# Two units of a graph layer's aggregation, one after the other or matmul by matmul in turn

## The reference

```python
h = relu(layernorm(x))                        # over the nodes
q, k = einsum('c,bcn->bn', wq, h), einsum('c,bcn->bn', wk, h)
scores = q[:, None, :] + k[:, :, None]        # then leaky relu, slope 0.01
att = softmax(scores, axis=-1)                # 1024 x 1024 a batch
agg = einsum('bcn,bmn->bcm', h, att)
out = x + relu(einsum('oc,bcm->bom', adj, agg) + bm)
```

## Time and profile before

| | |
|---|---|
| Time, median of 3 runs | 2122.78 us (2120.24 to 2122.8) |
| Profiled execution: time, span | 2123.36 us, 2121.6 us |
| TensorE matmuls busy | 2055.9 us (97%), 11312 instructions |
| VectorE busy | 1640.8 us (77%) |
| ScalarE busy | 1219.2 us (57%) |
| GpSimd busy | 390.6 us (18%) |
| Mean granted TensorE clock | 0.993 of full |

### The profile page before, as it was taken

The page is one execution under the profiler, slowest core; times in us unless marked ns, Lnnn a source line. Parts: engine busy times, 40 slices in busy tenths (PEclk is TensorE's granted clock), DMA queues, the critical chain, the costliest instruction groups (busy, mean ns, idle before and its releaser), DMA issues.

```text
span 2121.6 us, 35163 instructions
## 1 busy us (share of the span) xinstructions
PE 2055.9 (97%) x11312; PEld 960.5 (45%) x11312; DVE 1640.8 (77%) x3661; ACT 1219.2 (57%) x1873; POOL 390.6 (18%) x266
## 2 busy tenths in 40 slices
PE   4599999999999999999999999999999999999999
PEld 2244444444444444444444444444444444444444
DVE  6777788778888778787777887787887777877753
ACT  3565555655646665556655556555566655566543
POOL 0012211112212112111122211122111122111221
PEclk9799999999999999999999999999999999999999
DMA  5265544555544565444565445555445654445541
GB/s 169 91 149 140 125 106 144 134 149 139 117 102 152 128 156 135 100 123 140 139 148 120 118 129 136 144 139 118 105 149 129 154 134 104 120 143 139 114 100 40
DMA packets 178624, 271.51 MB, mean 128 GB/s; under 512 B 87648, under 2 KB 87648, under 8 KB 170336
## 3 DMA queue, kind: packets, MB, share of 16 engines
q1 hardware_dynamic: 178528, 270.59, 50.1%
HBM read 202.91 MB, written 67.63 MB: 128 GB/s over the span
## 4 chain that ended last, share of the span: by engine, by line
PE 80%; DVE 10%; issue 7%; DMA 1%; ACT 1%; SPq 0%; DVEq 0%; POOLq 0%
PE mix L338 15%; PE mix L339 15%; PE mix L340 15%; PE mix L319 10%; PE mix L321 10%; PE mix L320 10%; DVE den_out L612 4%; DVE p_ring L632 4%; PE small L302 2%; DVE p_lo L639 2%; DMA ab_rows<-ab_col 1%; DMA wm_nat<-in_adj_dram 0%; ACT v_hi L426 0%; DVE v_lo L644 0%; DMA ab_row<-ab_rows 0%
## 5 line engine op out<-in xcount | busy, mean ns | idle before, releaser
L338 PE MATMUL mix<-p_hi,v_hi 128*128 128x512 f16 x2048 | 777.2, 379 | 10.1 <-DVE p_lo L639 10.1
L339 PE MATMUL mix<-p_lo,v_hi 128*128 128x512 f16 x2048 | 776.9, 379 | 0.0
L340 PE MATMUL mix<-p_hi,v_lo 128*128 128x512 f16 x2048 | 776.8, 379 | 0.0
L736 POOL TENSOR_TENSOR res<-res,y 128x512 f32<-128x512 f32 x256 | 386.1, 1508 | 1710.2 <-ACT y L433 1710.2
L414 ACT ACTIVATE p_ring<-ab_row,cols 128x512 f32<-128x512 f32 x512 | 349.4, 692 | 181.4 <-DVE p_lo L639 155.4
L632 DVE SCALAR_TENSOR_TENSOR p_ring<-ab_row,cols,p_ring 128x512 f32<-128x512 f32 x512 | 376.7, 747 | 77.1 <-ACT p_ring L414 46.5
L319 PE MATMUL mix<-wmT_hi,h_hi 128*128 128x512 f16 x1024 | 389.2, 380 | 0.0
L321 PE MATMUL mix<-wmT_hi,h_lo 128*128 128x512 f16 x1024 | 389.1, 380 | 0.0
L320 PE MATMUL mix<-wmT_lo,h_hi 128*128 128x512 f16 x1024 | 389.1, 380 | 0.0
L612 DVE SCALAR_TENSOR_TENSOR den_out<-den_row,cols 128x512 f32<-128x512 f32 x512 | 371.6, 762 | 0.0
L422 ACT ACTIVATE p_hi<-p_ring 128x512 f16<-128x512 f32 x512 | 303.2, 592 | 87.3 <-DVE p_ring L632 69.9
(11 more groups left out here) (56 smaller groups left out, 782.2 us busy)
## 6 DMA issues: line engine op xcount, KB each, us to landing
xs<-in_x_dram SPq DMA_DIRECT2D x128, 512.0 KB, 6.1
res<-in_x_dram SPq DMA_DIRECT2D x256, 256.0 KB, 3.5
out_dram<-res SPq DMA_DIRECT2D x256, 256.0 KB, 2.5
den_row<-den_rows SPq DMA_DIRECT2D x32, 1024.0 KB, 4.6
ab_row<-ab_rows SPq DMA_DIRECT2D x32, 1024.0 KB, 6.8
wm_nat<-in_adj_dram SPq DMA_DIRECT2D x1, 1024.0 KB, 9.7
den_rows<-cols SPq DMA_DIRECT2D x32, 8.0 KB, 1.6
ab_rows<-ab_col SPq DMA_DIRECT2D x32, 8.0 KB
```

The costliest lines, as they stand in the source:

```text
L338: pe.matmul(ps[:, :], v_hi[:, nt, chans], p_hi[:, hf, nt, :], start=(nt == 0), stop=False)
L339: pe.matmul(ps[:, :], v_hi[:, nt, chans], p_lo[:, hf, nt, :], start=False, stop=False)
L340: mm = pe.matmul(ps[:, :], v_lo[:, nt, chans], p_hi[:, hf, nt, :], start=False, stop=(nt == NT - 1))
L736: pool.tensor_tensor(res[:, k, :], res[:, k, :], y[:, k % 2, :], ALU.add).then_inc(s_add, 1)
```

## The change

`unit` becomes `unit_pair`: units k and k + 1 run together. In each node tile the two take turns matmul by matmul, in two banks, with the same moving tile of p and different weight tiles of v. Both banks are waited for ahead of the pair, and each unit raises `s_acc` with its last matmul. The number of matmuls is the same, and so is their order within a unit; no other engine's program is touched.

```diff
-            def unit(b, k):
-                hf, ot = divmod(k, OT)
-                if k < MIX:
-                    pe.wait_ge(s_vlo[k % 2], cnt(b, NT // 2, (k + MIX) // 2 + 1))
-                else:
-                    pe.wait_ge(s_y[k % 2], cnt(b, U // 2, (k - MIX) // 2 + 1))
-                ps, chans = mix[k % MIX], slice(ot * P, (ot + 1) * P)
+            def unit_pair(b, k):
+                hf = k // OT
+                pair = (k, k + 1)
+                for u in pair:
+                    if u < MIX:
+                        pe.wait_ge(s_vlo[u % 2], cnt(b, NT // 2, (u + MIX) // 2 + 1))
+                    else:
+                        pe.wait_ge(s_y[u % 2], cnt(b, U // 2, (u - MIX) // 2 + 1))
                 for nt in range(NT):
                     if k == 0:
                         pe.wait_ge(s_vlo[nt % 2], cnt(b, NT // 2, nt // 2 + 1))
-                    if ot == 0:
+                    if k % OT == 0:
                         pe.wait_ge(s_plo, cnt(b, G, NT * hf + nt + 1))
-                    pe.matmul(ps[:, :], v_hi[:, nt, chans], p_hi[:, hf, nt, :], start=(nt == 0), stop=False)
-                    pe.matmul(ps[:, :], v_hi[:, nt, chans], p_lo[:, hf, nt, :], start=False, stop=False)
-                    mm = pe.matmul(ps[:, :], v_lo[:, nt, chans], p_hi[:, hf, nt, :],
-                                   start=False, stop=(nt == NT - 1))
-                mm.then_inc(s_acc, 1)
+                    for v, p in ((v_hi, p_hi), (v_hi, p_lo), (v_lo, p_hi)):
+                        for u in pair:
+                            ot = u % OT
+                            mm = pe.matmul(mix[u % MIX][:, :], v[:, nt, ot * P:(ot + 1) * P], p[:, hf, nt, :],
+                                           start=(nt == 0 and v is v_hi and p is p_hi), stop=(nt == NT - 1 and v is v_lo))
+                            if nt == NT - 1 and v is v_lo:
+                                mm.then_inc(s_acc, 1)
 
             def period(b, one, two):
-                for k in range(U):
-                    unit(b, k)
+                for k in range(0, U, 2):
+                    unit_pair(b, k)
```

## The result

The kernel with pairs takes 2139.6 us (median of 4 runs, 2138.99 to 2140.6), the kernel before on the same chip 2121.59 (4 runs, 2120.24 to 2122.8): ratio 1.0086, interval 1.0073 to 1.0098. It is 0.86% slower; 0.46% faster was forecast, 2111.9 us with 2109 to 2117 as the range. The profiled execution has a span of 2137.3 us, 15.7 more than before. Among the runs of this document two stand apart, and no ratio uses them: one of experiment 12 (2193.22 us, mean granted clock 0.945) and one of the kernel before, beside experiments 5 to 8 (5528.27 us).

What follows compares the result with a forecast made beforehand. TensorE paced the kernel at 63.87 us a batch, with 10.9 us lost waiting for `p_lo` 15. Passes -10.7, start -1.2 and end +1.05 summed to -10.9: 2111.9 us, range 2109 to 2117.

Steps and rivals of the forecast that it cites:

- The wait for `p_lo` 15: TensorE's unit 4 waits for VectorE's last `p_lo` in 13 batches; pairing removes it, 10.9 us, taken as 10.7.
- banks taken in turn: TensorE's matmuls alternating between two PSUM banks; no cost in pace assumed, 0 us.
- first mark: First projection group (L302) on TensorE, closing the start; 1.2 us gain kept there.
- the end: Last residual add on GpSimd, now behind unit 6's add because units 6 and 7 end together; cost 1.05 us.
- The chain relu 6, `h_hi`, `h`, `h_lo`: ScalarE and VectorE work behind unit 6; in B ends +45.8 from unit 0's start, 0.8 us before TensorE wants it.
- B: The second batch of a VectorE loop pass, without the jump; VectorE 3 us earlier, nothing waits.
- rival 2: In B, the chain from relu 6 to `h_lo` is late for the projection; 2136 us, chance 0.04.
- What is late next: TensorE's projection wants `h_lo` at +46.6; in A it ends +46.2, 0.4 us cover; 0.2 us taken off the gain.
- A: The first batch of a VectorE loop pass, where VectorE stands 2.20 us at its jump back and TensorE waits 0.7 us.
- SP and POOL: GpSimd's adds, stores and `write_ab_rows` go back some 1.5 us in B; 5 us to spare, no cost.
- Rival 1: Projection's wait for `h_lo` in A replaces the removed wait; 2116 us in part (chance 0.11), 2122 if nearly all.
- rival 3: Banks in turn cost TensorE pace (2173 us) or clock (2740 us); chance 0.03.

Runs made afterwards that it cites:

- experiment 12: Kernel before with only units 4 and 5 paired, add 3 held until the row scales are done, add 4 until the layer norm's scales: 2109.03 us, ratio 0.994.
- experiments 5 to 8: Four follow-up kernels run as one group with the kernel before on the same chip, whose median there was 2122.07 us.
- experiment 1: Changed kernel with all four pairs, GpSimd's adds cut to 8 of 512 columns: 2110.63 us, ratio 0.9939.
- 2: Kernel before, no pairs, with GpSimd's adds cut to 8 of 512 columns: 2111.99 us, ratio 0.9947.
- experiment 10: Kernel before, no pairs, with add 3 alone held until VectorE's row scales are done: 2112.03 us, ratio 0.9952.
- 5: Kernel before, no pairs, with add 2 held until unit 3 ends, so adds 2 and 3 go together: 2128.07 us, ratio 1.0031.
- experiment 7: Changed kernel with add 2 held until the next weights' denominators are done and add 4 until the normaliser's scales are: 2122.96 us, ratio 1.0008.
- experiment 8: Kernel before with only units 4 and 5 paired, and add 4 held until the layer norm's scales are done: 2109.46 us, ratio 0.9941.
- 9: Changed kernel with add 2 held until the row scales are done and add 4 until the layer norm's scales are: 2142.5 us, ratio 1.0093.
- experiment 11: Changed kernel with 9's holds on adds 2 and 4, and `write_ab_rows` moved ahead of store 2: 2134.67 us, ratio 1.0064.

## Why the prediction was wrong

**Right.** The wait for `p_lo` 15 is gone, and banks taken in turn cost TensorE nothing (0.2158 us a matmul). The relus are let go at +10.35, +20.7 and +31.06, as worked out. From unit 0 to the first mark 1.22 us are gained (1.2 forecast), and the end costs 1.08 (1.05); what the first mark gains is lost again behind it, by a fall of the clock that no term had. The chain relu 6, `h_hi`, `h`, `h_lo` in B ends at +45.80 in experiment 1, the very number of the sum; rival 2 didn't occur. Without the adds the total is 2110.63, and 2112.2 with the 1.6 us given back that the two last adds then lack; forecast 2111.9. Where no add is in the way, the kernel does what the sum said; what was left out turned the sign.

**The step that failed** is in "What is late next": "none of it starts later by the change, if ScalarE's queue lets it". VectorE's chain to `h_lo` was taken from the earlier trace rows and held to be the same length, with ScalarE as the only way in. It starts when it may, but got longer: by 46.19 to 47.53 = 1.34 us in A and by 3.26 in B. The cause lies in "SP and POOL": GpSimd's adds were followed as far as the stores behind them and the rows that these let go, and no price was put on the add for the engine beside it. The cover was 0.4 us in A and 0.8 in B; it went in all batches.

**A step before it was thin.** `p_lo` 15 at +25.9 was read as VectorE's own pace behind its jump. It held 0.65 us of a denominator that waited for an add. A step takes 2.60 us and the last one, which makes no new weight, 1.95 (1069.50 to 1071.44 in B); in A the meeting filled that one up to 2.61, so that eight steps of 2.6 looked even. (`p_lo` 11 of B, counted back in steps of 2.6, is at +12.5 and not at "about +12"; nothing hung on it.) Looking at each L612 in A would have shown one of 1.40 us among the 0.74s, with an add across it, and with that the question what the moved adds would meet.

**The rivals.** Rival 1, the projection's wait in place of the other, named the right wait, but stopped at "nearly all of the gain given back" (2122), in A only. It had no reason for B, and none for a lateness that grows with the moved relus. The loss went past it on three items: 0.97 us in the A batches (12.6), 0.54 in the B batches (8.1), and 6.6 where the clock fell behind the wait. The last had its wrong place in rival 3. Its rule from the Trainium skill ("TensorE: Matmul & The Clock Gate", psum-queue depth-cycling) put the falls on banks; experiment 1 has the same order of banks and no fall in 29 batches, so in this kernel they come with the projection's wait.

**The size.** With the work of the adds out of the way, the pairs save 1.4 us (experiments 1 and 2), not 10.9: nearly all of the 10.9 was add 3's, and moving this add alone gives it back (experiment 10).

**What stays open.** That the adds' place is the cause is shown from both sides: adds made tiny (1, 2), adds moved into the way (5), adds moved out of it (7, 8, 10). The version with all four pairs, the full adds, and nothing in the way was not reached: 9 and 11 keep `h_lo` in time but make `ab_row` late, and the rows of 11 show what stands before the row's load but no run takes it away. Why the clock falls behind some of the waits and not behind most (4 of the 13 of 0.8 us) isn't settled.

## What to carry to other kernels

When an edit moves the release of an instruction, follow it through every engine that runs from it, and ask at each what it will then lie across, not only what stands behind it. Read single durations of one line and not its mean: one instruction at twice its usual length shows two engines on one path, and it says which of them sets the time. Here holding one add for a few microseconds, on an engine that is busy 19% of the span, gives 12.6 us with one pair (experiment 8) and 10.2 with none, against 18.0 lost by four pairs without it.

## What the runs showed of the hardware

- Some of the smallest instructions are held for nearly the whole of an add: 128x4 tiles take 1.23 us (`var_eps`) and 1.16 (`t_y`) instead of 0.17 and 0.16, beside an add of 1.26. Others aren't: `moments` keeps its 0.20 us. It goes both ways: an add issued inside a denominator takes 1.62 us, and the pair of adds 3.38 instead of 2.5.
- `p_lo` and `p_ring` with one operand in PSUM pass beside an add of 1.27 us at 0.69 and 0.75 us.
- The write of `ab_rows`, 8 KB, takes 11.0 us from issue to landing in the kernel after (median), the 1 MB load of `ab_row` 7.2; a store issued 1.5 us behind such a write took 11 us (experiment 11), where the median in the kernel before is 2.5.
- TensorE's clock fell to the lower level behind an idle time of 0.8 us with 64 matmuls of four columns after it, for seven or eight matmuls of 512, in 4 of the 13 batches where both stood in a row, and behind none of the waits of 0.37 us in the kernel after; in experiment 7 it fell once behind a wait of 0.50.
